# A transformer decoder on one core: queries rotated behind the keys' chunking, and three other moves in the attention stages

## What is computed

```python
x = _layernorm(x + _L0_attn_ref(x, ...), axis=-1)             # ternary weights, rotary, 16 heads of 8, chunked
x = _layernorm(x + _L0_xattn_ref(x, ctx_512, ...), axis=-1)
x = _layernorm(x + _L0_ffn_ref(x, ...), axis=-1)
x = _layernorm(x + _L1_attn_ref(x, ...), axis=-1)             # a scan, not an attention
x = _layernorm(x + _L1_xattn_ref(x, ctx_512, ctx_512, ...), axis=-1)
x = _layernorm(x + _L1_ffn_ref(x, ...), axis=-1)
x = _layernorm(x + _L2_attn_ref(x, ...), axis=-1)             # 16 heads, keys turned by a learned product
...

def rotary(t, n):                                             # of the first self attention
    t1, t2 = (t[..., ::2], t[..., 1::2])
    return jnp.concatenate([t1 * c - t2 * s, t1 * s + t2 * c], axis=-1)
```

## Time and profile before

| | |
|---|---|
| median of 3 runs | 1634.43 us (1632.85 to 1637.06) |
| the profiled execution's own time | 1637.46 us |
| its span from first to last instruction | 1635.5 us |
| PE busy | 1443.3 us, 88% |
| DVE busy | 1047.1 us, 64% |
| ACT busy | 667.0 us, 41% |
| POOL busy | 218.7 us, 13% |
| mean granted TensorE clock | 0.947 of 2.4 GHz |

### The profile page before, as it was taken

The page is one execution under the profiler, slowest core; times in us unless marked ns, Lnnn a source line. Parts: engine busy times, 40 slices in busy tenths (PEclk is TensorE's granted clock), DMA queues, the critical chain, the costliest instruction groups (busy, mean ns, idle before and its releaser), DMA issues. The chain is left out here.

```text
span 1635.5 us, 22279 instructions
## 1 busy us (share of the span) xinstructions
PE 1443.3 (88%) x8409; PEld 681.9 (42%) x8409; DVE 1047.1 (64%) x2625; ACT 667.0 (41%) x952; POOL 218.7 (13%) x235
## 2 busy tenths in 40 slices
PE   2898889996778889999899999999998879999886
PEld 2232444443553434446444333436444633335444
DVE  6796655457975677774555696365854666774555
ACT  3466443223325023332553466443323345554433
POOL 3000000001000433343000000000000012332002
PEclk9899899997889889999999899899999889999998
DMA  5000000003000010000002000000001000000000
GB/s 225 1 1 1 1 1 1 1 0 151 1 1 1 1 52 1 1 1 1 1 1 113 1 1 1 1 1 1 1 0 78 0 1 1 1 2 1 1 1 13
DMA packets 4105, 27.15 MB, mean 17 GB/s; under 512 B 416, under 2 KB 2464, under 8 KB 2976
## 3 DMA queue, kind: packets, MB, share of 16 engines
q1 hardware_dynamic: 4000, 25.74, 4.0%
HBM read 25.21 MB, written 0.52 MB: 16 GB/s over the span
## 5 line engine op out<-in xcount | busy, mean ns | idle before, releaser
L954 DVE TENSOR_REDUCE maxima<-banks 128x1 f32<-128x512 f32 (+4 forms) x640 | 363.0, 604 | 122.5 <-PE banks L801 116.3
L1126 ACT ACTIVATE big<-banks 128x1024 f32<-128x1024 f32 (+2 forms) x320 | 294.3, 960 | 264.0 <-PE banks L844 94.0
L829 PE MATMUL banks<-big 32*128 32x512 f32 (+6 forms) x1280 | 231.2, 610 | 17.0 <-DVE big L975 12.6
L801 PE MATMUL banks<-big 32*128 32x77 bf16 (+6 forms) x1024 | 156.8, 289 | 16.1 <-DVE maxima L954 4.6
L867 PE MATMUL banks<-big,v_heads 128*9 128x512 f32 (+7 forms) x1024 | 158.9, 567 | 6.3 <-ACT heads_out L1014 3.2
L1743 DVE TENSOR_TENSOR big<-big,banks 128x512 f32<-128x512 f32 (+1 forms) x116 | 79.8, 688 | 115.1 <-PE banks L1594 95.2
L1719 ACT ACTIVATE big<-banks 128x512 f32<-128x512 f32 (+1 forms) x116 | 69.0, 595 | 146.8 <-PE banks L1593 146.6
L801 PEld LDWEIGHTS banks<-big 32*128 32x128 bf16 (+1 forms) x1024 | 55.9, 94 | 165.9 <-DVE maxima L954 91.7
L1624 PE MATMUL banks<-big,moe_weights 128*128 128x512 f32 (+1 forms) x232 | 120.0, 601 | 3.4 <-DVE big L1752 3.4
L613 POOL TENSOR_TENSOR rstd<-mean_var,minus_half 128x4 f32<-128x4 f32 x34 | 35.3, 1037 | 592.9 <-DVE mean_var L530 592.9
L829 PEld LDWEIGHTS banks<-big 32*128 32x128 f32 (+3 forms) x1280 | 72.5, 177 | 70.0 <-ACT big L1126 23.6
(11 more groups left out here) (429 smaller groups left out, 2152.6 us busy)
## 6 DMA issues: line engine op xcount, KB each, us to landing
moe_weights<-in_moe SPq DMA_DIRECT2D x1, 4864.0 KB, 14.5
moe_weights<-in_moe SPq DMA_DIRECT2D x1, 4768.0 KB, 22.8
moe_weights<-in_moe SPq DMA_DIRECT2D x1, 3264.0 KB, 10.4
moe_weights<-in_l3x SPq DMA_DIRECT2D x1, 3072.0 KB, 10.2
late_weights<-in_l2x SPq DMA_DIRECT2D x1, 2048.0 KB, 7.6
moe_weights<-in_l SPq DMA_DIRECT2D x1, 1234.0 KB, 13.0
rows<-in_rows SPq DMA_DIRECT2D x1, 1152.0 KB, 8.1
late_weights<-in_turned SPq DMA_DIRECT2D x1, 1152.0 KB, 17.7
```

Of the source, the lines that this page charges most:

```text
L801: last = nc.tensor.matmul(RING[n % NR][:, x * klen:x * klen + last_key(t)], q[rows, t * P:(t + 1) * P], ks[rows, 0:last_key(t)], start=Tru ...
L829: last = nc.tensor.matmul(SC[pair % 2][0:size, j % 2, n0:S], ks[rows, i * P:i * P + size], q[rows, n0:S], start=True, stop=turned)
L954: nc.vector.tensor_reduce(dst, src, AX_X, ALU.max).then_inc(ring_free.up(), 1)
L1126: nc.scalar.activation(E[pair % NEP][0:size, :, n0:S], SC[pair % 2][0:size, :, n0:S], ACT.Exp, scale=scale).then_inc(exp_ready.up(), 1)
```

## The change

Four edits. (1) In `begin` POOL waits for `keys_cut_dve` (DVE's nine key pieces) where it waited for `projected`; what it does is the same. (2) In `cross_attention_8`, where `prior.summed` holds, the four query tiles of the first half stand ahead of the context's six projections and all ten are early; `needs` becomes 10 for the whole first half, in layer 0's cross attention as well, whose list stays as it was. (3) In `row_attention`, the early projections of a block whose prior is summed go round banks 2 to 5. That is layer 1's cross attention and both attentions of layer 3. (4) In `layer2_attention` the first half's four value tiles stand ahead of `qf`, the keys and the queries.

```diff
@@ row_attention
-    project_banks = [4 + n % 2 if n < early else 2 + n % 4 for n in range(len(projections))]
+    project_banks = [4 + n % 2 if n < early and not prior.summed else 2 + n % 4 for n in range(len(projections))]
@@ begin, gpsimd
-            pool.wait_ge(projected.sem, projected.at(1))
+            pool.wait_ge(keys_cut_dve.sem, keys_cut_dve.at(1))
             for b in range(B):
                 rotate(nc.gpsimd, pool_step, c.XN, slice(b * ST, (b + 1) * ST), cos, sin, False, c.big1).then_inc(queries_rotated.up(), 1)
@@ cross_attention_8
-    projections = [context_tile(c, wk, ctxT, K, k, bias=c.ninth[:] if bk is None else col(bk, k)) for k in range(4)]
-    projections += [natural(c, ctxT[:, b * SK:(b + 1) * SK], wv, v[:, b, :, 0:8], 8, row=bv) for b in range(B)]
-    projections += [tiles_of(c, wq, c.XT, Q, k, b, bias=col(bq, k)) for b in range(B) for k in range(4)]
-    needs = {(b, k): 7 + 4 * b + k for b in range(B) for k in range(4)}
+    context = [context_tile(c, wk, ctxT, K, k, bias=c.ninth[:] if bk is None else col(bk, k)) for k in range(4)]
+    context += [natural(c, ctxT[:, b * SK:(b + 1) * SK], wv, v[:, b, :, 0:8], 8, row=bv) for b in range(B)]
+    first, second = ([tiles_of(c, wq, c.XT, Q, k, b, bias=col(bq, k)) for k in range(4)] for b in range(B))
+    summed = kwargs["prior"].summed
+    projections = (first + context if summed else context + first) + second
+    needs = {(b, k): 11 + k if b else 10 for b in range(B) for k in range(4)}
@@ the attention_8 call
-    ... early=6, late=10, dense=10,
+    ... early=10 if summed else 6, late=10, dense=10,
@@ layer2_attention
         if half:
             late = len(projections)
+        else:
+            projections += values
@@
-            if k == (1 if half else 3):
+            if half and k == 1:
                 projections += values
```

More of the change, by code:

```diff
@@ L1521, in cross_attention_8 @@
     col = lambda bias, k: None if bias is None else bias[:, k:k + 1]
-    projections = [context_tile(c, wk, ctxT, K, k, bias=c.ninth[:] if bk is None else col(bk, k)) for k in range(4)]
-    projections += [natural(c, ctxT[:, b * SK:(b + 1) * SK], wv, v[:, b, :, 0:8], 8, row=bv) for b in range(B)]
-    projections += [tiles_of(c, wq, c.XT, Q, k, b, bias=col(bq, k)) for b in range(B) for k in range(4)]
-    needs = {(b, k): 7 + 4 * b + k for b in range(B) for k in range(4)}
-    return attention_8(c, [SK], 8.0 ** -0.5, projections=projections, needs=needs, ones=v[:, :, :, 8], early=6, late=10, dense=10,
+    context = [context_tile(c, wk, ctxT, K, k, bias=c.ninth[:] if bk is None else col(bk, k)) for k in range(4)]
[4 more added lines that the diff above has]
+    needs = {(b, k): 11 + k if b else 10 for b in range(B) for k in range(4)}
+    return attention_8(c, [SK], 8.0 ** -0.5, projections=projections, needs=needs, ones=v[:, :, :, 8], early=10 if summed else 6, late=10, dense=10,
                        finish=lambda: Norms(c, product_of(c, c.yT8, wo), [norm], c.X, row=bo, front=Front(c.Y8, c.yT8[:, 0])), **kwargs)
```

## The result

| | before | after |
|---|---|---|
| median | 1635.59 us (6 runs, 1630.75 to 1637.06) | 1619.42 us (6 runs, 1615.27 to 1620.69) |
| ratio | | 0.9908, 95% interval 0.9896 to 0.9919 |
| the profiled execution's own time | 1637.46 us | 1620.12 us |
| its span | 1635.5 us | 1618.3 us |
| mean granted TensorE clock | 0.947 | 0.952 |

By the ratio the change made the kernel 15.0 us faster (0.0092 of 1634; the two medians lie 16.2 apart), where -5.7 was forecast and 1624 was the lower end of the range. Timed again beside other kernels it gave 1619.64 against 1633.63, ratio 0.9913 (0.9901 to 0.9926). The sign was right; the gain is more than twice what the sum holds. Layer 3's attentions, which the outline of what is computed leaves out of those that matter, turn out to have the largest part in the miss.

The account below looks back on a forecast made before the run. PE was busiest overall, but each place was judged by the engine waited for: DVE's key chain in the first block, PE in projections. Terms -4.1 + 0 + 0 - 0.4 - 1.2 = -5.7 gave 1628.7 us, range 1624 to 1633.

Parts of the forecast that it names:

- the sum: Whole kernel: first block -4.1, layer 0 0, layer 1 0, layer 2 -0.4, layer 3 -1.2, together -5.7 us.
- All four rivals: Clock eats more, 1631.7 (20%); POOL ends first block, 1632.3 (8%); keys not slowed by POOL, 1633.7 (4%); rival 4.
- The first block: Start: with POOL behind the cut, DVE's rotation and key pieces run faster, -4.1 us; bounds 4.4 and 2.2 of gain.
- I take -2.0: Layer 1's cross attention: gain taken between -0.8 (clock rises as late as now) and -3.4 (clock high from the start).
- Two of four at the low level cost 2 x 0.96: Layer 1's second half: light work ahead puts two of its four products at the low clock, bringing layer 1 to 0.
- -3.0 for the old fall: Layer 2's attention: value tiles leave the place ahead of the clock's fall at 899.9; -3.3 at most, 3.0 taken.
- +2.2 for a new one at the head: Layer 2's attention: light products now at the head may make the clock fall there, +2.2 us.
- +0.4 for the order: Layer 2's attention: last two query products lose their cover and the turn comes 0.4 later, +0.4 us.
- the -2.9 of my lower bound: Layer 2's attention: the case with no clock fall at the head, -2.9 us, against -0.4 forecast.
- Together -1.2; bounds 0 and -1.5: Layer 3's two attentions: four banks remove waits, -0.6 us in each, -1.2 in all.
- rival 4: Layers 1 and 2: clock falls once more in each and stays low into the score rounds; +4.4, 1638.8 us (8%).
- 3.0 us off for before's long execution: Whole kernel: the median of the runs lies 3.0 us below the profiled execution, so the forecast starts from 1634.4.

Follow-up runs that it names:

- Experiment 4: The whole change plus two or four gate and up products of layer 2's experts computed twice: 1628.59 us with two, 1620.26 us with four.
- both_spread: The whole change with layer 1's context projections and layer 2's value tiles spread among the heavy products: 1620.21 us, ratio 0.9924.

## Why the prediction was wrong

The traces' 16.1 us are 10.4 more than the sum: 4.2 of them in layer 3's attentions and what follows them, 2.2 in layer 2, 2.0 in layer 1 and 1.5 at the end of layer 0's attention, for which the sum had nothing (the last 0.5 are scattered). All four rivals had less gain than the forecast, or a loss.

- **The first block: right.** Forecast of -4.1, traces -4.2, timed alone -5.2. The 1 us more may be the end of layer 0's attention: 82.7 in all twelve traces with the new wait, 84.1 to 85.8 in three of eight with the old one. That link was seen, not tested. The mechanism, two engines that slow each other in the same operands, is as described: DVE's pieces 0.30 each for 0.55, its multiplications 2.49 for 4.09. The Trainium skill's page "SBUF — State Buffer", section "SBUF: two separate sides", has an exclusive lock between the two engines; the traces agree in kind. Read strictly, as the prediction worked out, a multiplication alone would have taken 0.4 us; it took 0.62.
- **Layer 1, "I take -2.0 ... Two of four at the low level cost 2 x 0.96. Sum 0": the size was off.** The block takes 52.5 in the mean of eleven traces with the new order and four banks, 54.3 in seven with the old one: -1.8. Products at the low clock behind the light work came as forecast in eight of the eleven, in the other three (those with 50.9) none. What failed is the -2.0, a middle between -0.8 and -3.4: the clock was high from the first product in every trace with the new order and low there or within 3 us in all seven with the old, and in the first trace of after the first product behind `xT` came 4.2 us sooner, more than the -3.4 that I had kept as the bound.
- **Layer 2, -3.0 for the old fall, +2.2 for a new one at the head, +0.4 for the order: the fall at the head did not come.** In none of the ten traces with this order is there one. Measured -2.6 in the table, near the -2.9 of my lower bound. The other reading was right in part: of the two low stretches of the old order (11 and 25 us behind the piece's start) one is left, 22 us behind it.
- **Layer 3, "Together -1.2; bounds 0 and -1.5": the step that failed most.** It prices four banks at the waits that go, as if nothing behind them changed. The waits are as sized (18.1 for 18.5 us in the projections' own part, 44.4 for 45.0), but alone and in the whole the banks give 4.4 to 5.4 us. What the runs show in place of the term: where the work enters as in after, the clock does not fall in the 40 us behind the shorter waits (3 us) nor in the last piece (1.3). Why is not shown; that denser products keep it up is contradicted by the traces that enter otherwise.
- **The sum itself.** It takes everything outside the edited stages as fixed. Experiment 4 shows that this does not hold: 1.7 us of extra work changed unedited pieces by 10.5, 3.4 us changed none. Moving the start by 4 us and each later stage by 2 us may do the same; that was not tested apart. In this kernel's favour, all four edits together land in the execution with the short lengths nearly every time (eleven timed runs from 1615.3 to 1620.7), while three of the four edits without layer 1's or layer 2's land there in two or three of twelve. That is why the two parts are worth 8 us each only when the others are there, and it may be most of the 3 to 4 us by which the whole is more than its parts. No rival had this; rival 4 had the chain of falls, but as a loss.
- **The median.** I took 3.0 us off for before's long execution; that was right, and I should have drawn more from it: two traces of one program would have shown before the forecast that a low stretch in one trace is no property of the program.

The trace does not bear out that falls come from long idle gaps, as the Trainium skill's page "TensorE: Matmul & The Clock Gate" has it in the section "HAM oscillation — how this bites in real kernels": the clock fell at 901.2 in after behind a stretch with PE busy 10.11 us of 10.20. The same page's section "What's actually happening" says that the same kernel shows a different number of slow products from run to run, by the phase of the clock gate at its start. The traces agree in kind, with 1629.6, 1633.4 and 1635.5 us for three executions of before, but the differences arise all along the program.

What stays open: why some placements of the work lead to the long pieces, in terms that would let one compute them beforehand; and whether the order in layer 1 has a worth of its own beyond 2 us apart from where it puts later work. Splitting layer 3's gain between its two attentions was not tried, nor were the banks timed where the work enters with the long piece.

## What to carry to other kernels

Where TensorE's granted clock changes often, trace the unchanged kernel two or three times before pricing an edit, and call a low stretch removable only if it comes back in each. A removed wait in the middle of matrix products can be worth more than its own length where products behind it have stood at the low clock (here 1.2 us of waits were worth 5), but that is no rule to add up by: in other placements of the same code the traces do not show it. And when parts are timed alone, time the whole with one part left out as well: parts worth 0 and 1.6 alone were worth 8 each together.

## What was not expected of the hardware

- The length of a piece falls near a few values, and different kernels share them. Over the twenty traces the piece ahead of layer 3's attentions took 90.5 to 90.7 us thirteen times, 91.1 twice and 93.5 to 93.9 five times; the last piece took 83.6 nine times, 84.9 four times, 86.1 to 86.4 six times and 88.7 once. A reason that fits, argued and not tested: work that reaches a low stretch later does less of itself at half speed, so executions that enter apart leave closer together.
- 1.7 us of added work on PE in a stretch at the high clock cost 7 to 9 us, 3.4 us cost 1 to 2.
- Where the piece ahead of it took 90.5 to 90.7, layer 3's first head took 48.6 us with waits for banks of some tenths of a us between its first products, 0.4 in all, and 45.5 without them; where it took 93.5 to 93.9, the head without these waits was the longer one (47.9 to 49.6 for 46.2 and 46.3).
- Light products mixed in between heavy ones (two 64-row or 77-column products behind each 128-row one) did not keep the clock up behind them in layer 1 of `both_spread`: it was low for the 10 us that followed (PE busy 7.12 us of 7.90 ahead of it). In layer 2, spread in the same manner, no low stretch followed in either trace.
